# Where the free rows of the second routed group get their zeros: eight fills from one queue, or seven indexed sends from another

## The reference

```python
x = x + _L0_xattn_ref(ctx_1024, _layernorm(x, axis=-1), L0_xattn_conv_w, L0_xattn_conv_b, 512, 512, 4)
x = x + _L0_ffn_ref(_layernorm(x, axis=-1), ...)   # 8 experts, top 2, hidden 128, and a shared expert
x = x + _L1_xattn_ref(_layernorm(x, axis=-1), ctx_1024, ctx_1024, ...)   # attention, 16 heads of 64
x = x + _L1_ffn_ref(_layernorm(x, axis=-1), ...)   # 8 experts, top 2, hidden 384, gated
```

```python
activation = jnp.sqrt(jax.nn.softplus(logits))
top_vals, top_idx = jax.lax.top_k(activation, K)
combine = jnp.sum(jax.nn.one_hot(top_idx, E, dtype=X.dtype) * top_vals[..., None], axis=-2)
hdn = jax.nn.silu(jnp.einsum('nd,edh->enh', Xf, rW1) + rb1[:, None, :])
y = jnp.einsum('enh,ehd->end', hdn, rW2) + rb2[:, None, :]
routed = jnp.einsum('ne,end->nd', cf, y).reshape(B, T, d)
```

## Time and profile before

| what | value |
|---|---|
| median of 3 runs | 827.2 us (826.39 to 827.79) |
| the profiled execution: its own time | 822.08 us |
| the profiled execution: its span, first to last instruction | 820.2 us |
| granted clock of TensorE, mean | 0.980 |
| TensorE busy | 749.1 us, 91% of the span |
| VectorE / ScalarE / GpSimd busy | 530.4 / 489.3 / 429.7 us |
| data moved | 154.47 MB, 188 GB/s over the span |

### The profile page before, as it was taken

One profiled execution on the slowest core, in us unless ns is written; L12 is line 12 of the kernel. 1 busy time (PEld: TensorE's weight loads), 2 busy tenths in 40 slices (PEclk: granted clock), 3 DMA queues, 4 the chain that ended last, 5 costly groups with the idle time before them and its releaser, 6 DMA issues.

```text
span 820.2 us, 16199 instructions
## 1 busy us (share of the span) xinstructions
PE 749.1 (91%) x4633; PEld 653.7 (80%) x4633; DVE 530.4 (65%) x1423; ACT 489.3 (60%) x1379; POOL 429.7 (52%) x399
## 2 busy tenths in 40 slices
PE   4799987889898499999999999789999999999996
PEld 3546635676776399999998988689999999999995
DVE  5687857552665488888889888776543343365454
ACT  2337735555676488888877787356555454454541
POOL 3000655564687958888545778544652445333220
PEclk9899999999999799999999999899999999999998
DMA  8999997787899943663610444633444434565457
GB/s 248 343 285 308 332 300 257 241 276 227 184 268 241 320 121 81 163 153 70 210 63 2 161 163 148 206 104 120 140 137 142 144 104 133 179 210 177 161 178 233
DMA packets 128745, 154.47 MB, mean 188 GB/s; under 512 B 10875, under 2 KB 118550, under 8 KB 127638
## 3 DMA queue, kind: packets, MB, share of 16 engines
q1 hardware_dynamic: 102896, 112.55, 44.7%
q0 software_dynamic: 18624, 34.29, 15.8%
q10 hardware_dynamic: 7142, 6.59, 2.4%
HBM read 77.39 MB, written 76.00 MB: 187 GB/s over the span
## 4 chain that ended last, share of the span: by engine, by line
PE 70%; DVE 8%; issue 5%; ACT 5%; POOL 5%; DMA 4%; DVEq 1%; another core or an unknown queue 0%; SPq 0%; POOLq 0%; ACTq 0%
PE psum L849 24%; PE psum L1164 9%; PE psum L1142 8%; PE psum L1236 7%; PE psum L1241 6%; PE psum L1237 6%; POOL X L718 4%; PE psum L1152 3%; PE psum L1252 3%; ACT pr L1549 2%; PE psum L1215 2%; DMA X<-yl_dram,slots_y 1%; DMA yk_dram<-ys,L 1%; PE psum L1037 1%; PE psum L942 1%
## 5 line engine op out<-in xcount | busy, mean ns | idle before, releaser
L771 POOL DMA_INDIRECT yk_dram<-ys,L x52 | 53.6, 1031 | 136.2 <-ACT ys L1641 136.0
L718 POOL DMA_INDIRECT X<-yl_dram,slots_y x64 | 101.0, 1578 | 31.9 <-issue 14.2
L690 POOL DMA_INDIRECT xs_dram<-N,slots x64 | 65.9, 1029 | 97.0 <-DVEq L1943 58.4
L1549 ACT ACTIVATE pr<-psum,nmx 128x64 f32<-128x64 f32 x512 | 108.4, 365 | 6.8 <-DVE nmx L2314 6.6
L1236 PE MATMUL psum<-whi,xTh 128*128 x284 | 103.9, 366 | 3.4 <-ACT xTh L1603 2.4
L2410 DVE TENSOR_TENSOR hs<-psum,hs 128x384 f32<-128x384 f32 x71 | 39.7, 559 | 87.4 <-PE psum L1241 45.2
L1237 PE MATMUL psum<-wlo,xTh 128*128 x284 | 96.0, 338 | 0.0
L759 POOL DMA_INDIRECT xs_dram<-N,slots x64 | 69.7, 1090 | 35.9 <-ACT ys L1641 19.1
L1241 PE MATMUL psum<-whi,xTl 128*128 x284 | 74.1, 342 | 1.5 <-DVE xTl L2433 1.4
L751 POOL TENSOR_TENSOR pr<-pr,sm 128x1024 f32<-128x1024 f32 x32 | 62.2, 1944 | 19.5 <-DVE sm L2321 17.3
L1633 ACT ACTIVATE hs<-psum 128x384 f32<-128x384 f32 x71 | 34.9, 492 | 49.0 <-PE psum L1241 36.7
(11 more groups left out here) (370 smaller groups left out, 2041.2 us busy)
## 6 DMA issues: line engine op xcount, KB each, us to landing
fx<-xs_dram SPq DMA_DIRECT2D x78, 130.0 KB
yl_dram<-fy SPq DMA_DIRECT2D x78, 128.0 KB
xs_dram<-fill SPq DMA_DIRECT2D x4, 2340.0 KB, 14.1
xs<-xs_dram SPq DMA_DIRECT2D x71, 130.0 KB
wlo<-in_L_ffn_W_dram SPq DMA_DIRECT2D x4, 1536.0 KB, 11.4
xs_dram<-cz SPq DMA_DIRECT2D x1, 5070.0 KB, 24.2
xs_dram<-cz SPq DMA_DIRECT2D x7, 650.0 KB
X<-in_x_dram SPq DMA_DIRECT2D x4, 1024.0 KB, 11.7
```

What stands on the lines that cost most here:

```text
L690: po.indirect_dma_start(XS, bass.IndirectOffsetOnAxis(ap=slot[k][:, t:t + 1], axis=0), N0[:, t, :], None).then_inc(s[done], 16)
L718: po.indirect_dma_start(X[:, t, :], None, YL[b // 2], bass.IndirectOffsetOnAxis(ap=slot_y[k][:, t:t + 1], axis=0), compute_op=ALU.add).the ...
L771: po.indirect_dma_start(YK, bass.IndirectOffsetOnAxis(ap=yid[:, j:j + 1], axis=0), ys[j % YB], None).then_inc(s[f"y_out{j % YB}"], 16)
L1549: last = act(pr[b][:, S * h:S * h + S], bank[2 * b + h // 8][:, S * (h % 8):S * (h % 8) + S], ACT.Exp, bias=nmx[:, h:h + 1])
```

## The change

The eight fills of group two in the fold are gone. Instead, VectorE finds the 896 free rows of group two in two small steps, in slots 5 and 8 of group one's loop (`padding(0)` and `padding(1)`, on tiles of 8, 56 and 7 numbers per partition). POOL writes 128 rows of zeros to them by each of seven indexed sends (`PADS = 7`). These stand in `send_rows(1)` between the sends to the first experts and those to the second ones. SP waits for them (`padded`) before it loads group two's slots. Beside that, the stores of `st_r` share semaphores in pairs (i // 2), so ScalarE waits for two stores of pair j - 3 where it waited for one, and POOL makes a small table of numbers, `pad_no`, at the start.

```diff
-        names = """... l1_in zeroed0 zeroed1
+        names = """... l1_in zeroed pads padded
@@ SP, in the fold
-            sp.dma_start(rows_of[0], zeros.to_broadcast([P, LS, XW])).then_inc(s["zeroed0"], 16)
+            sp.dma_start(XS[0:LS * P, :].rearrange("(p r) d -> p r d", p=P), zeros.to_broadcast([P, LS, XW])).then_inc(s["zeroed"], 16)
@@
-                sp.dma_start(rows_of[1][:, parts[j]:parts[j + 1], :],
-                             zeros.to_broadcast([P, parts[j + 1] - parts[j], XW])).then_inc(s["zeroed1"], 16)
@@ SP, routed_rows
                 if g:
+                    sp.wait_ge(s["padded"], 16 * PADS)
                     sp.dma_start(vraw, VD[0].rearrange("p (m c) n -> p m (c n)", c=2)).then_inc(s["v_in"], 16)
@@ POOL
+            po.iota(pad_no, pattern=[[P, PADS]], base=0, channel_multiplier=1, allow_small_or_imprecise_dtypes=True)
@@ POOL, send_rows
-                po.wait_ge(s[f"zeroed{g}"], 16 * (1, PAIRS)[g])
+                if g == 0:
+                    po.wait_ge(s["zeroed"], 16)
@@
+                if g:
+                    po.wait_ge(s["pads"], 1)
+                    for i in range(PADS):
+                        po.indirect_dma_start(
+                            XS, bass.IndirectOffsetOnAxis(ap=pad_at[:, i:i + 1], axis=0),
+                            zero4, None).then_inc(s["padded"], 16)
@@ ACT, fold
-                        ac.wait_ge(s[f"st_out{i}{j % DEEP}"], 16 * (j // DEEP))
+                        ac.wait_ge(s[f"st_out{i // 2}{j % DEEP}"], 16 * 2 * (j // DEEP))
@@ VectorE
+            def padding(part):
+                base, e_ = LS * P, E * LT
+                counts, cum, open_, at = (ta[:, 2 * E * k:2 * E * k + E] for k in range(4))
+                at = at[:, 0:PADS]
+                c3 = wk12[:, 0:PADS * E].rearrange("p (i e) -> p i e", e=E)
+                if part == 0:
+                    last_t = tc_[:, e_:2 * e_].rearrange("p (e t) -> p e t", e=E)[:, :, LT - 1:LT]
+                    nc.vector.tensor_copy(counts.rearrange("p (e a) -> p e a", a=1), last_t)
+                    ve.drain()
+                    nc.vector.tensor_tensor_scan(cum, ones8[:, :], counts, 0.0, ALU.mult, ALU.add)
+                    ve.drain()
+                    tt(cum, counts, cum, ALU.subtract)
+                    ve.drain()
+                    stt(open_, te[:, :], float(P), cum, ALU.mult, ALU.add)
+                    ve.drain()
+                else:
+                    tt(c3, bc(pad_no, E), rep(open_, PADS), ALU.is_ge)
+                    ve.drain()
+                    tt(c3, c3, rep(counts, PADS), ALU.mult)
+                    ve.drain()
+                    nc.vector.tensor_reduce(at, c3, AX.X, ALU.add)
+                    ve.drain()
+                    stt(pad_at, at, float(base), pad_no, ALU.add, ALU.add)
+                    ve.drain()
+                    ve.sem_inc(s["pads"], 1)
@@ VectorE, routed
                     nc.vector.tensor_copy(fxT[j % 4].rearrange("p c n -> p (c n)"), turned_at(j)).then_inc(s["f_xt"], 1)
+                    if j in (5, 8):
+                        padding(j // 8)
```

More of the change, by code:

```diff
@@ L87 @@
 DEEP = 3
+PADS = LS - 2 * LT
 XB, YB = 8, 4
@@ L167, in build @@
         sm = [sb(f"sm{k}", [P, NHEAD]) for k in range(2)]
+        pad_no, pad_at = nmx[:, 0:PADS], sm[0][:, 0:PADS].bitcast(I32)
         xstats = sb("xstats", [P, TILES, 6])
@@ L307, in build @@
         VD = nc.dram_tensor("vw_dram", [NB, P, PAIRS, D], F32).ap()
-        names = """consts ctx_in u_in x_in0 x_in1 x_in2 x_in3 s_in0 s_in1 s_in2 s_in3 wq_in kvo_in w_in0 w_in1 w_in2 w_in3 w_hi w_lo cols_in rest_in cw_in l1_in zeroed0 zeroed1
+        names = """consts ctx_in u_in x_in0 x_in1 x_in2 x_in3 s_in0 s_in1 s_in2 s_in3 wq_in kvo_in w_in0 w_in1 w_in2 w_in3 w_hi w_lo cols_in rest_in cw_in l1_in zeroed pads padded
             u_c_in mid_in
-            pre_c_tp pre_c_sb wqt_p wqt_sb k_p k_sb v_p v_sb a_p vw_p st_sb st_out00 st_out01 st_out02 st_out10 st_out11 st_out12 st_out20 st_out21 st_out22 st_out30 st_out31 st_out32
+            pre_c_tp pre_c_sb wqt_p wqt_sb k_p k_sb v_p v_sb a_p vw_p st_sb st_out00 st_out01 st_out02 st_out10 st_out11 st_out12
             b2_in b2_lo b2_zero sw_in rw_in
@@ L416, in _ @@
             zeros = zero4[:, :].rearrange("p (a d) -> p a d", a=1)
-            rows_of = [XS[LS * P * g:LS * P * (g + 1), :].rearrange("(p r) d -> p r d", p=P) for g in range(LG)]
-            parts = [LS * i // PAIRS for i in range(PAIRS + 1)]
             sp.wait_ge(s["kvo_in"], 16 * 3)
@@ L438, in _ @@
                         sp.dma_start(AD[:, :, i, P * j:P * j + P].rearrange("b p n -> p b n"),
-                                     st_r[i][j % DEEP].rearrange("p (b n) -> p b n", b=NB)).then_inc(s[f"st_out{i}{j % DEEP}"], 16)
+                                     st_r[i][j % DEEP].rearrange("p (b n) -> p b n", b=NB)).then_inc(s[f"st_out{i // 2}{j % DEEP}"], 16)
                     else:
@@ L442, in _ @@
                         sp.dma_start(VD[2 * h:2 * h + 2, :, j, :].rearrange("b p n -> p b n"),
-                                     st_r[i][j % DEEP].rearrange("p (b n) -> p b n", b=2)).then_inc(s[f"st_out{i}{j % DEEP}"], 16)
-                sp.dma_start(rows_of[1][:, parts[j]:parts[j + 1], :],
-                             zeros.to_broadcast([P, parts[j + 1] - parts[j], XW])).then_inc(s["zeroed1"], 16)
-            for i in range(4):
+                                     st_r[i][j % DEEP].rearrange("p (b n) -> p b n", b=2)).then_inc(s[f"st_out{i // 2}{j % DEEP}"], 16)
+            for i in range(2):
                 for d in range(DEEP):
-                    sp.wait_ge(s[f"st_out{i}{d}"], 16 * len(range(d, PAIRS, DEEP)))
+                    sp.wait_ge(s[f"st_out{i}{d}"], 16 * 2 * len(range(d, PAIRS, DEEP)))
             for c in range(DC):
@@ L1424, in shared_out @@
                 elif q == 2:
-                    ac.wait_ge(s["st_out00"], 16 * len(range(0, PAIRS, DEEP)))
+                    ac.wait_ge(s["st_out00"], 16 * 2 * len(range(0, PAIRS, DEEP)))
                 for h, k in enumerate((6, (5, 4)[q // LQ])):
```

## The result

The changed kernel took a median of 839.77 us (836.55 to 843.65, five runs), the kernel before 827.2 us beside it: 1.0139 of before, interval 1.0107 to 1.0171. The medians lie 12.6 us apart, and the changed kernel is outside my range.

What follows compares the result with a forecast made beforehand. It took the end to depend on when group one's last result, mostly after TensorE work, lets POOL gather. Terms -0.5 + 0 + 0 + 0.5 + 0 + 0 = 0 left the median at 827.2 us, range 823.2 to 830.2 us.

Steps and rivals of the forecast that it cites:

- the sends as traffic: Group one's loop, 165 to 196 us: 0.93 MB more, 4.0 us of transfers; range 0 to +4.0 us, taken +0.5 us.
- Seven sends on GpSimd: Group one's loop: 8.9 us of sends hidden by pace waits and POOL's idle time, 3.3 us left before the gathers; 0 us.
- The fills that go: Fold: 5.19 MB fewer transfers and 8.9 us of SP freed, no named waiter; 0 to -4.7 us, taken -0.5 us.
- TensorE's own work up to 138.83 us: Start of group one's loop: TensorE's earlier work hides the freed time, so earlier slot loads would not start it earlier.
- SP's loads of group two, hidden: After the last send: loads issued at 197.9 instead of 196.19 us, still ahead of TensorE's first turn at 207.24 us; 0 us.
- VectorE, 0 us: Slots 5 and 8 of group one's loop: 1.1 us of small instructions each, hidden; bounds 0 to +2.2 us.
- semaphores, 0 us: Fold's stores: ScalarE waits for a second store of the pair three back, but no store was waited for; 0 us.
- Freed transfers help: Rival, faster: relieved transfer engines remove a TensorE stop in the fold, 2.3 to 4.7 us, 822.5 to 824.9 us; chance 0.29.
- that stop: Fold: TensorE stands still 2.33 us ahead of 110.60 us without a named reason; full transfer engines might cause it.
- Traffic and pace: Rival, slower: added sends delay slot loads in group one's loop, up to 4.0 us, 828.8 to 831.2 us; chance 0.20.

Runs made afterwards that it cites:

- ordinary ones: Kernel before with fills and shared semaphores, plus seven sends of real rows to an unread table in group one's loop: 1.0010 on a quick chip, 1.0115 on a long one.
- zero ones: Kernel before with fills and shared semaphores, plus seven zero sends to fixed rows of an unread table, no VectorE steps: 1.0186 on a long chip.
- fills kept: Changed kernel with the fold's eight fills put back beside all the change adds: 1.0029 of before on a quick chip, 1.0133 on a long one.
- rows found alone: Kernel before with fills, plus VectorE's two steps, the numbers and shared semaphores, no zero sends: 0.9993 on a quick chip, 1.0016 on a long one.
- the changed kernel, a third time: Changed kernel word for word, timed beside the kernel before on a long chip (before 831.33 us): 1.0150 of before.
- the shared semaphores alone: Kernel before with only the semaphores of the fold's stores shared by two, on a quick chip (before 815.94 us): 1.0001 of before.
- paced: Changed kernel with all 39 sends of group two paced evenly by group one's slots, on a long chip: 1.0124 of before.
- last: Changed kernel with its seven zero sends moved behind the second expert's 16 sends: 1.0012 of before on a quick chip, 1.0140 on a long one.
- spread: Changed kernel with one zero send behind every second send of the second expert instead of one block, on a long chip: 1.0086 of before.

## Why the prediction was wrong

- **The term that failed is "the sends as traffic": +0.5 us, at most +4.0.** On long chips seven more sends cost 9.5 us (ordinary ones, 0.0115 x 829.33) to 15.5 us (zero ones, 0.0186 x 830.73; 12.9 us by the medians). They come not as waits for transfers, whose share fell (0.74 to 0.62), but with holds: ScalarE's waits for `fh` without a releaser went from 6.8 to 16.7 us in the loop on one long chip, and the granted clock from 0.95 to 0.87. On quick chips fills kept against rows found alone is 0.0036 x 816 = 2.9 us, two chips' ratios compared and hardly clear of their intervals, and the ordinary ones 0.8 us: inside my bound. That bound came from what transfers of this size take. I had one stop of TensorE for nothing that the trace names before me (2.33 us) and used it for the fills alone, not to bound the sends.
- **Seven sends on GpSimd, 0 us:** right, on either kind of chip, and for the reason given: GpSimd still waits for the last result (7.59 us and 5.89 us on long chips, 1.72 us on a quick one). The cover on a quick chip was thinner than my 3.3 us.
- **The fills that go, -0.5 us:** too small on quick chips. The changed kernel against the one with fills kept is (0.9961 - 1.0029) x 816 = -5.5 us. These are two chips' ratios, and by their intervals it could be 3 us less or more, so it is not sure to lie beyond my bound of -4.7. My cover, "TensorE's own work up to 138.83 us", is true on long chips (144.97 and 144.78 us, same loads) and false on quick ones, where TensorE waited 2.71 us for the slots. I had missed that fills lengthen the landing of the sends ahead of the loads. On a long chip it is 1.0150 without fills against 1.0133 with them: no gain that can be measured. The Trainium skill, "DMA: Bandwidth & Descriptors", section "Issuing engines are not separate DMA queues", says that transfers of SyncE and GpSimd run on the same 16 engines and interleave. The quick chips' traces agree: with fills in SyncE's queue the loads that wait for GpSimd's sends came 6.1 us after the last one, without them 2.6 us.
- **SP's loads of group two, hidden:** right; in the changed trace they are issued at 216.67 us and the first is turned at 228.39 us.
- **VectorE, 0 us; semaphores, 0 us:** right (1.0016 and 0.9993; 1.0001). Slot 5's and slot 8's instructions took 1.9 us, beside other work.
- **The rivals.** "Freed transfers help" is what happens on a quick chip, by another path than the stop ahead of 110.60 us, and that stop is not the fills' doing. It shows on long chips alone: TensorE stops there for 3.86 us without fills (the changed kernel, a third time), and for at most 0.8 us at a time there on a quick chip with them (the shared semaphores alone, 105 to 115 us). Fetched instructions do not explain the later holds either: in the changed trace no packet of an instruction queue moves between 170 and 190 us, while TensorE stands still twice. "Traffic and pace" had the sign of the first result and GpSimd's sends, but neither mechanism nor size, and pacing was tried and did not help.

So the result has two parts: about -4 to -6 us for the fold, which showed on the quick chips alone, and +9 to +15 us with the sends and their holds, which showed on the long chips alone. The holds' releaser is in no trace: the recorded end of a matmul is modelled, and a few records can be missing, so TensorE may have been working slowly, or its signal may have come late. That, and what sets the two kinds of chips apart, stays open. No version here beats the changed kernel on a quick chip, or the kernel before on a long one.

## What to carry to other kernels

Ask of a time which chip it is from: the same two kernels stood at 1.015 and at 0.996, each beside its own before, and a single comparison would have taught either rule. Work that is hidden on its own engine can still come with holds of another. Where a trace has waits without a releaser, name them as a risk of what you add, and test with a copy of it whose result nobody reads. And take a fill out of a dense stretch for what waits behind it in the queues, not only for who waits for the fill.

## What the runs showed of the hardware

- The kernel before takes 814 to 816 us on some chips and 827 to 831 us on others. Between 69 and 300 us VectorE and ScalarE have no wait of over 1.5 us without a releaser in any of the traces from quick chips; every trace from a long one has them (ScalarE's are up to 5.2 us).
- On long chips seven sends more of 130 KB come with more of such waits, in a block, paced or last (spread, 6.2 us): ScalarE's ahead of `fh` add up to 11.5 to 16.7 us in group one's loop, against 2.4 to 6.8 us without them. In the changed kernel's trace TensorE's granted clock goes from 1.00 to 0.50 within a stop of 5.05 us, and a pair of matmuls takes twice as long (0.60 us, then 1.21 us) until it returns.
- With a transfer of 5.19 MB ahead of 130 KB loads TensorE waited 11.46 us, with one of 10.4 MB ahead of the fold's stores 14.85 us.
